# A decoder layer on one core: input statistics moved to the opening, six products by C on GpSimd, pieces of the last chunk a step sooner, and loops in a block that is skipped

## The chip, the cores and the metric

The kernel runs on one core of a Trainium2 chip. The metric is the device time of one execution in microseconds. TensorE (PE) multiplies matrices into PSUM, VectorE (DVE), ScalarE (ACT) and GpSimd (POOL) work on rows of 128 partitions, and SyncE (SP) issues the DMAs here. The engines run on their own and wait for each other by semaphores alone.

## What is computed

One decoder layer on 2048 tokens of width 256, in float32:

```python
x = x + attn_ref(layernorm(x))        # a Mamba block, then RMS norm, a gelu FFN, RMS norm
x = x + xattn_ref(layernorm(x), ctx)  # cross attention, 16 heads, 1601 keys
x = x + ffn_ref(layernorm(x))         # soft mixture of 8 experts with 128 slots each
```

The Mamba block has 512 channels and 16 states each. Its core is

```python
dA = exp(delta[..., None] * A)
h = dA * h + (delta * u)[..., None] * B[:, None, :]
y = einsum('bdn,bn->bd', h, C) + u * D
```

The cross attention is softmax(q k^T / 4) v with q and k of 16 numbers a head. The kernel shifts all scores by one bound worked out from the lengths of q and k; if that bound is too loose (over 120), it works out a maximum for each query instead.

## The kernel before

**The loop.** Time is cut in 4 chunks of 512 tokens (c). A chunk has 32 steps, one for each pair of channel blocks (p) and state (n); a step's number over all chunks is w = 32 c + i, from 0 to 127, and w works on 128 partitions x 1024 columns (two channel blocks side by side). For each w:

- GpSimd, `scan_input(w)` (L648, the product in L662): du times B into `dbu[w % 3]` in SBUF, and from chunk 1 on one more column (L669). It waits until VectorE's product of step w - 3 is done.
- ScalarE, `decays(w)` (L848, exponentials in L856): two exponentials into two PSUM banks, of which there are two pairs (w % 2). Ahead of them stands `carry_over(w - 2)` (L837, copy in L843), which takes the last column of the state of step w - 2 and waits for VectorE's product of that step.
- VectorE, `scan(w)` (L1258, the scan in L1268): h = decay * h + input, written over the decays in PSUM; then `between(c, i)` (L1351), a fixed list of other work for step i; then `times_c(w)` (L1271, product in L1279): state times C into one of six SBUF buffers.
- TensorE, `add_states(j)` (L1938, matmuls in L1946): adds the states 2j and 2j + 1 by an identity matrix to the sum in PSUM, at step 2j + 3.
- SP loads B and C for two steps at a time (`load_b`, L546, `load_c`, L555), each spread over all partitions, when the buffer of two loads ago is free. In its queue also stand the store of the next chunk's B and C (`store_bc`, at i = 10 of a chunk) and stores of keys.

**Around the loop.** Each engine has a list, by i, of what else it does in a step, for other chunks: projections and convolution of chunk c + 1, output projection, norm and FFN of chunk c - 1. In chunk 0 keys and values of the attention are made (GpSimd's `key_rest`, L692), in the last chunk the queries of chunks 0 and 1. All of it is in program order, so an instruction that waits holds up everything behind it on its engine.

**Statistics of the input.** `norm_stats(c)` (L1172, four bn_stats in L1174), `norm_moments(c)` (L1176, four bn_aggr in L1180 and a memset) and `norm_variance(c)` (L1182, L1186) are VectorE's, `layer_norm_root(c)` (L645 inside) is GpSimd's, `input_shift(c)` (L1188, L1190) again VectorE's. For chunk 1 they stand in steps 1, 2 and 4 of chunk 0, for chunk c + 2 in steps 15, 16 and 20 of chunk c. All chunks use the same columns of `stat`, `mv`, `ve`, `rstd` and `crec`. Before the loop VectorE makes chunk 0's statistics, the convolution and the step size, ending with the first input.

**The last chunk.** At i = 16 TensorE turns h1 of chunk 2 (`turn_h1`); at i = 17 ScalarE copies it (`turned_h1`, L867). TensorE's `hidden` (L1992) runs two FFN blocks each at i = 17, 19, 21 and 24, ScalarE's gelus of them (L872) at 18, 20, 22 and 25. Gelu and Exp need different tables, so each change between them loads one (ACT_TABLE_LOAD). ScalarE's `turned_query` (L927) stands at i = 12 and 21.

**The loose bounds.** After the loop VectorE writes `loose` (L1518). TensorE, VectorE and SP each read it and run a block only if it is 1 (L2127, L1532, L604). In TensorE's block one loop runs over the 4 chunks, and what is inside (4 tiles x 16 heads x 4 matmuls) is written out. In VectorE's block a loop runs over the 16 tiles with 16 reductions written out. In the runs here `loose` is 0 and the blocks are skipped. Behind them the scores and the attention follow (L2156, L1101, L2169).

## Time and profile before

| what | value |
|---|---|
| median of 3 runs | 1351.25 us (1350.41 to 1352.27) |
| the profiled execution | 1352.97 us |
| its span in the profile | 1351.2 us |
| busy: TensorE, its weight loads, VectorE, ScalarE, GpSimd | 1224.3, 641.3, 744.7, 929.5, 384.4 us |
| mean granted TensorE clock | 0.958 of full speed |
| opening / loop / rest up to the attention | 0 to 40 / 40 to 613 / 613 to 682 us |
| attention / experts | 682 to 1097 / 1097 to 1351 us |

How to read it: times are in us from the span's start. A row of instructions in order of time gives start, duration, engine, line, operation, what is written and read, and in brackets the idle time of the engine ahead of it and what ended it. "issue" is a wait for which the profile shows no releaser. Matmuls overlap each other, and a float32 one counts as two. Register and branch instructions aren't counted as busy, so a jump shows as idle time. Idle time of an engine that isn't the late one costs nothing.

### The profile page before, as it was taken

What the parts mean: (1) busy time and instruction counts of PE and PEld (TensorE: products, weight loads), DVE (VectorE), ACT (ScalarE), POOL (GpSimd) and SP (SyncE); (2) the same over time, 40 slices, a digit from 0 to 9 for tenths busy, and PEclk for the clock granted to TensorE, in tenths of its full rate; (3) what the DMA queues carried; (4) which work ended last, traced back from release to release, by engine and by line L of the source; (5) the groups of instructions that cost most, each with busy time, mean ns of one, the idle gap of its engine ahead of it and who ended that gap; (6) DMA issues with size and microseconds to landing.
All of it is one profiled execution on the core that took longest, in us unless ns stands there. A gap on an engine that the chain in (4) does not pass through costs nothing.

```text
span 1351.2 us, 19337 instructions
## 1 busy us (share of the span) xinstructions
PE 1224.3 (91%) x7848; PEld 641.3 (47%) x7848; DVE 744.7 (55%) x829; ACT 929.5 (69%) x1213; POOL 384.4 (28%) x280
## 2 busy tenths in 40 slices
PE   8679987998978897899979999999999999999999
PEld 4234543444443453355623333333333345588988
DVE  4999999999999999983352001001001237640011
ACT  5867756677657854662379999999989967742300
POOL 2646766666556765750000000000001000000000
PEclk9789988999988998999979999999999999999999
DMA  6534665243324432449461000000000000203501
GB/s 183 176 110 122 230 219 192 94 152 128 111 86 144 133 131 106 160 151 256 104 166 25 1 2 2 1 2 1 2 2 1 1 32 0 94 1 161 244 16 47
DMA packets 43033, 128.02 MB, mean 95 GB/s; under 512 B 6103, under 2 KB 21400, under 8 KB 39545
## 3 DMA queue, kind: packets, MB, share of 16 engines
q1 hardware_dynamic: 42942, 126.75, 29.0%
q8 instruction: 64, 1.05, 0.3%
q14 instruction: 27, 0.22, 0.1%
HBM read 109.64 MB, written 17.09 MB: 94 GB/s over the span
## 4 chain that ended last, share of the span: by engine, by line
PE 41%; ACT 26%; DVE 22%; issue 9%; DMA 1%; DVEq 0%; SPq 0%; POOL 0%; ACTq 0%
ACT arena L1101 18%; DVE ps L1268 13%; PE ps L2169 4%; PE ps L2300 4%; PE ps L2343 4%; PE ps L2156 4%; PE ps L2228 4%; PE ps L1946 4%; DVE arena L1279 4%; PE ps L2007 3%; PE ps L1992 2%; PE ps L2318 2%; ACT ps L856 2%; PE ps L2331 2%; PE ps L1726 2%
## 5 line engine op out<-in xcount | busy, mean ns | idle before, releaser
L1101 ACT ACTIVATE arena<-ps,bound 128x1536 f32<-128x1536 f32 (+1 forms) x278 | 403.9, 1559 | 13.1 <-PE ps L2156 12.7
L662 POOL TENSOR_TENSOR arena<-arena 128x1024 f32<-128x1024 f32 x127 | 298.3, 2350 | 217.5 <-DVE arena L1279 181.8
L1268 DVE TENSOR_TENSOR_SCAN ps<-ps,arena 128x1024 f32<-128x1024 f32 x128 | 300.6, 2349 | 9.2 <-ACT ps L856 7.8
L2156 PE MATMUL ps<-arena 97*32 97x512 bf16 x3264 | 239.2, 385 | 18.8 <-ACT arena L1101 12.9
L1946 PE MATMUL ps<-arena,ident 128*128 128x512 f32 x512 | 238.3, 611 | 3.9 <-DVE arena L1279 3.9
L2169 PE MATMUL ps<-arena 128*32 128x512 f32 (+1 forms) x1664 | 227.5, 598 | 3.1 <-DVE arena L1587 2.6
L856 ACT ACTIVATE ps<-arena 128x512 f32<-128x512 f32 x256 | 166.2, 682 | 52.0 <-DVE arena L1279 47.6
L2156 PEld LDWEIGHTS ps<-arena 97*32 97x32 bf16 (+1 forms) x3264 | 84.0, 96 | 211.9 <-ACT arena L1101 125.4
L645 POOL TENSOR_TENSOR rstd<-ve,mhalf 128x4 f32<-128x4 f32 (+3 forms) x23 | 25.5, 1110 | 495.7 <-DVE ve L1559 421.5
L1279 DVE TENSOR_TENSOR arena<-ps,arena 128x1024 f32<-128x1024 f32 x128 | 156.0, 1219 | 9.5 <-DMA arena<-bc_scratch 1.9
L1946 PEld LDWEIGHTS ps<-arena,ident 128*128 128x128 f32 x512 | 99.5, 197 | 125.9 <-issue 119.1
L1587 DVE STREAM_TRANSPOSE arena<-ps 128x512 f32<-128x512 f32 x16 | 11.5, 717 | 206.9 <-PE ps L2169 206.9
L843 ACT ACTIVATE arena<-ps 128x2 f32<-128x2 f32 x96 | 16.4, 171 | 116.2 <-DVE arena L1279 116.2
L2169 PEld LDWEIGHTS ps<-arena 128*32 128x32 f32 (+1 forms) x1664 | 54.1, 111 | 48.0 <-DVE arena L1587 7.5
L1992 PE MATMUL ps<-arena 128*128 128x512 f32 x128 | 59.7, 614 | 14.7 <-ACT arena L872 7.6
L1546 DVE TENSOR_TENSOR xt<-xt,ps 128x512 f32<-128x512 f32 x8 | 5.5, 688 | 116.0 <-PE ps L2174 116.0
L1873 PE MATMUL ps<-arena 128*128 128x512 f32 x128 | 61.3, 625 | 6.5 <-ACT arena L772 3.7
L2007 PE MATMUL ps<-arena 128*128 128x256 f32 x256 | 58.4, 382 | 3.2 <-ACT arena L872 3.2
L2228 PE MATMUL ps<-arena 128*128 128x512 f32 x128 | 57.7, 593 | 0.4 <-ACT arena L1125 0.4
L2300 PE MATMUL ps<-arena 128*128 128x257 f32 x256 | 55.8, 380 | 0.0
L2343 PE MATMUL ps<-arena 128*128 128x256 f32 x256 | 55.4, 379 | 0.0
L2007 PEld LDWEIGHTS ps<-arena 128*128 128x128 f32 x256 | 47.9, 190 | 14.5 <-ACT arena L872 4.8
(205 smaller groups left out, 1384.2 us busy)
## 6 DMA issues: line engine op xcount, KB each, us to landing
arena<-bc_scratch SPq DMA_DIRECT2D x128, 512.0 KB, 4.2
arena<-in_mw SPq DMA_DIRECT2D x16, 1024.0 KB, 10.3
qx_scratch<-arena SPq DMA_DIRECT2D x48, 128.0 KB, 3.3
arena<-qx_scratch SPq DMA_DIRECT2D x4, 1536.0 KB
arena<-kx_scratch SPq DMA_DIRECT2D x1, 4803.0 KB
kx_scratch<-arena SPq DMA_DIRECT2D x36, 128.0 KB, 4.7
arena<-vx_scratch SPq DMA_DIRECT2D x1, 3328.0 KB
vx_scratch<-arena SPq DMA_DIRECT2D x6, 512.0 KB, 5.1
```

What stands on the lines that cost most here:

```text
L662: product = pool.tensor_tensor(dbu[:, w % DR], du[:, DP * p:DP * p + DP], over(bg[:, w // BG % 2, n % BG], DP), ALU.mult)
L856: act.activation(decay_bank(w, x), delta[:, d], ACT.Exp, scale=neg_a[:, d, n:n + 1]).then_inc(S["da_ready"], 1)
L1101: act.activation(flat(prob[k % PSLOTS])[0:n, 0:w], banks(SPAN * (k % 2), SPAN)[0:n, 0:w], ACT.Exp, bias=bound[0:n, 3:4], scale=HD ** -0.5) ...
L1268: dve.tensor_tensor_scan(decay_banks(w), decay_banks(w), flat(dbu[:, w % DR]), carry[:, DP * p, n:n + 1], ALU.mult, ALU.add).then_inc(S["s ...
L1279: dve.tensor_tensor(state(w), ps[:, 2 + DP * (w % 2):2 + DP * (w % 2) + DP, :], over(cg[:, w // BG % 2, n % BG], DP), ALU.mult).then_inc(S ...
L1946: last = mm(bank(x), ident[:, :], state(2 * j + s)[:, x], start=False, stop=(j % HP == HP - 1 and (j in SUMMED or s == 1)))
L2007: last = mm(acc, gate[:, f, tok(i)], w2[:, f], start=(f == 0), stop=(c == NC - 1 and f == FB - 1))
L2156: last = mm(ps[r:r + w, SPAN * (k % 2) + s % SPAN, :], kx[0:XR + 1, head, b * P + r:b * P + r + w], qx[0:XR + 1, c, head, :], start=True, ...
L2169: last = mm(ps[2 * HD * x:2 * HD * x + 2 * HD, 6, :], vx[0:n, b, G * g + x, :], prob[s // SPAN % PSLOTS][0:n, s % SPAN], start=(b == 0), s ...
L2228: last = mm(bank(2 * (t % 2) + n), xnt[:, t % 2, k], snt[DK * k + n], start=(k == 0), stop=(k == DK - 1))
L2300: last = mm(ps[:, 4 + x if x < 4 else x - 4, 0:DM + 1], lg[:, t, tok(x)], xn[:, t, :], start=(t == 0), stop=(t == TT - 1))
L2343: last = mm(ps[:, t % 8, 0:DM], cwt[:, t, tok(x)], eo[:, x], start=(x == 0), stop=(x == NE - 1))
```

## The change

Four things, in one diff.

1. The statistics of chunks 1 and 2 are made before the loop: VectorE runs `norm_stats`, `norm_moments` and `norm_variance` for both behind `conv_keep(0)`, with the wait for all of x ahead of them; GpSimd runs both roots before the loop. Each chunk now has columns of its own in the small arrays. Chunk 3's stay at steps 15 and 16 of chunk 1. The counts that wait for `prep_dve` go up by 2.
2. In steps 19, 50, 53, 66, 82 and 85 (`POOLED`) the scan writes its state over its input in `dbu` in SBUF, VectorE makes no product, and GpSimd multiplies by C, in its queue just ahead of its input for step w + 3. ScalarE's carry copy of such a step waits for the scan alone and reads `dbu`. A new semaphore `pc_ready` counts GpSimd's products, and whoever waited for `hc_ready` waits by the two counts `by_vector` and `by_pool`.
3. In the last chunk ScalarE's `turned_h1` stands at i = 16 instead of 17, its gelus at 17, 19, 22 and 25 instead of 18, 20, 22 and 25, its `turned_query` at 11 and 20 instead of 12 and 21; TensorE's `hidden` at 17, 18, 21 and 24 instead of 17, 19, 21 and 24.
4. In TensorE's block for loose bounds three loops are nested (chunk, tile, pair of heads) around two heads written out, 8 matmuls; VectorE raises `nm_ready` by 2 inside its own block for it.

```diff
-SUMMED = []
+POOLED = [19, 50, 53, 66, 82, 85]
...
+        def by_vector(w):
+
+            return w - by_pool(w)
+
+        def by_pool(w):
+
+            return sum(v < w for v in POOLED)
...
                 if q >= 2:
-                    sp.wait_ge(S["hc_ready"], BG * (q - 1))
+                    sp.wait_ge(S["hc_ready"], by_vector(BG * (q - 1)))
+                    if by_pool(BG * (q - 1)):
+                        sp.wait_ge(S["pc_ready"], by_pool(BG * (q - 1)))
...
-                if w >= DR:
-                    pool.wait_ge(S["hc_ready"], w - DR + 1)
+                if w >= DR and w - DR in POOLED:
+                    pool.wait_ge(S["pc_ready"], by_pool(w - DR + 1))
+                    if w - DR < NW_ALL - NU:
+                        pool.wait_ge(S["carry_done"], w - DR + 1)
+                elif w >= DR:
+                    pool.wait_ge(S["hc_ready"], by_vector(w - DR + 1))
...
+            def times_c(w):
+
+                n = step(w)[2]
+                pool.wait_ge(c_in[w // BG % 2], 16 * (w // BG // 2 + 1))
+                pool.wait_ge(S["y_acc"], w // 2 - RING + 1)
+                pool.wait_ge(S["scan_done"], w + 1)
+                pool.tensor_tensor(state(w), dbu[:, w % DR], over(cg[:, w // BG % 2, n % BG], DP),
+                                   ALU.mult).then_inc(S["pc_ready"], 1)
...
+            pool.wait_ge(S["vx_init"], 6)
+            for c in (1, 2):
+                layer_norm_root(c)
             for c in range(NC):
                 for i in range(NU):
                     w = c * NU + i
+                    if w - DR in POOLED:
+                        times_c(w - DR)
                     if w:
                         scan_input(w)
...
             def carry_over(w):
                 c, p, n = step(w)
-                act.wait_ge(S["hc_ready"], w + 1)
+                if w in POOLED:
+                    act.wait_ge(S["scan_done"], w + 1)
+                    last = dbu[:, w % DR, :, C - 1:C]
+                else:
+                    act.wait_ge(S["hc_ready"], by_vector(w + 1))
+                    last = ps[:, 2 + DP * (w % 2):2 + DP * (w % 2) + DP, C - 1:C]
...
-                    if i == (20 if more else 17) and c:
+                    if i == (20 if more else 16) and c:
                         turned_h1(c - 1)
...
-                    if i in (18, 20, 22, 25) and not more:
-                        hidden(c - 1, 2 * (18, 20, 22, 25).index(i))
+                    if i in (17, 19, 22, 25) and not more:
+                        hidden(c - 1, 2 * (17, 19, 22, 25).index(i))
...
-                        if i in (12, 21):
-                            turned_query(i // 21)
+                        if i in (11, 20):
+                            turned_query(i // 20)
...
                 dve.wait_ge(S["da_ready"], DP * (w + 1))
-                dve.tensor_tensor_scan(decay_banks(w), decay_banks(w), flat(dbu[:, w % DR]),
+                states = flat(dbu[:, w % DR]) if w in POOLED else decay_banks(w)
+                dve.tensor_tensor_scan(states, decay_banks(w), flat(dbu[:, w % DR]),
                                        carry[:, DP * p, n:n + 1], ALU.mult, ALU.add).then_inc(S["scan_done"], 1)
...
                 if c == 0:
-                    if i == 1:
-                        norm_stats(1)
-                    if i == 2:
-                        norm_moments(1)
-                        norm_variance(1)
                     if i == 4:
                         input_shift(1)
...
                 if c + 2 < NC:
-                    if i == 15:
+                    if i == 15 and c:
                         norm_stats(c + 2)
-                    if i == 16:
+                    if i == 16 and c:
...
             conv_keep(0)
+            dve.wait_ge(S["w_mamba"], 16 * 3)
+            for c in (1, 2):
+                norm_stats(c)
+                norm_moments(c)
+                norm_variance(c)
...
                 between(w // NU, w % NU)
-                times_c(w)
+                if w not in POOLED:
+                    times_c(w)
...
-                        if i in (17, 19, 21, 24):
-                            f = 2 * (17, 19, 21, 24).index(i)
+                        if i in (17, 18, 21, 24):
+                            f = 2 * (17, 18, 21, 24).index(i)
...
                 with pe.Fori(0, NC) as c:
-                    for i in range(CT):
-                        for h in range(NH):
-                            if h >= 2:
-                                pe.wait_ge(S["nm_ready"], (c * CT + i) * NH + h - 1)
-                            for j, (o, n) in enumerate(KCOLS):
-                                last = mm(ps[:, 4 * (h % 2) + j, 0:n], head_queries(0, XR, c, h, tok(i)), kx[0:XR, h, o:o + n],
-                                          start=True, stop=True)
-                            last.then_inc(S["ms_ps"], 1)
-                        pe.wait_ge(S["nm_ready"], (c * CT + i) * NH + NH)
+                    with pe.Fori(0, CT) as i:
+                        with pe.Fori(0, NH // 2) as g:
+                            for x in range(2):
+                                pe.wait_ge(S["nm_ready"], c * (CT * NH) + i * NH + g * 2 + x + 1)
+                                queries = qx[0:XR, bass.ds(c, 1), bass.ds(g * 2 + x, 1), bass.ds(i * P, P)]
+                                for j, (o, n) in enumerate(KCOLS):
+                                    last = mm(ps[:, 4 * x + j, 0:n], queries.rearrange("p a b c -> p (a b c)"),
+                                              kx[0:XR, bass.ds(g * 2 + x, 1), o:o + n].rearrange("p a b -> p (a b)"),
+                                              start=True, stop=True)
+                                last.then_inc(S["ms_ps"], 1)
+                        pe.wait_ge(S["nm_ready"], c * (CT * NH) + i * NH + NH + 2)
```

## Rows read from the trace of the kernel before

**Rows 1.** The page, busy us (share of the span) and instructions of each engine.

```profile
PE 1224.3 (91%) x7848; PEld 641.3 (47%) x7848; DVE 744.7 (55%) x829; ACT 929.5 (69%) x1213; POOL 384.4 (28%) x280
```

**Rows 2.** Stretches: length; busy (count) of PE, PEld, DVE, ACT, POOL; PE clock, DMA share, GB/s.

```profile
142.00:284.00 142.00, 119.26 (x323) 61.33 (x321) 139.95 (x111) 93.50 (x176) 93.21 (x63) 0.89 0.53 175
284.00:311.00 27.00, 21.87 (x50) 8.98 (x49) 25.05 (x17) 26.09 (x41) 16.72 (x13) 1.00 0.44 135
...
323.00:355.00 32.00, 31.72 (x108) 19.34 (x109) 30.30 (x21) 17.66 (x39) 21.58 (x17) 1.00 0.39 132
...
429.00:445.00 16.00, 16.00 (x39) 6.87 (x38) 15.63 (x11) 15.70 (x24) 11.34 (x9) 1.00 0.42 144
```

**Rows 3.** Scan, VectorE's product (ns min/median/max), GpSimd's (busy, mean ns | idle).

```profile
L1268 DVE TENSOR_TENSOR_SCAN ps<-ps,arena x128: 2342/2349/2359, 40.5 to 604.7; 128x1024 f32<-128x1024 f32 x128
...
L1279 DVE TENSOR_TENSOR arena<-ps,arena x128: 1199/1222/1227, 42.9 to 607.1; 128x1024 f32<-128x1024 f32 x128
...
L662 POOL TENSOR_TENSOR arena<-arena 128x1024 f32<-128x1024 f32 x127 | 298.3, 2350 | 217.5 <-DVE arena L1279 181.8
```

**Rows 4.** Chunk 0: TensorE in order of time, and the chain's last piece there.

```profile
92.64 0.60 PE L1742 MATMUL ps<-sel,arena 128*128 128x8 f32 x2 [7.00 <-ACT arena L781]
...
119.34 3.45 PE ps L1946 x8
```

**Rows 5.** The last chunk: TensorE in order of time, the chain's last addition, and a wait.

```profile
541.87 1.04 PE L1726 MATMUL ps<-ident,arena 128*128 128x128 f32 x8
...
551.39 5.40 PE L1992 MATMUL ps<-arena 128*128 128x512 f32 x8 [5.05 <-ACT arena L867]
...
605.96 7.08 PE ps L1946 x16
...
DVE ps L1268 <- ACT ps L856: 4.0, 4, 1.5
```

**Rows 6.** VectorE in steps 1 and 2, in order of time.

```profile
44.07 2.35 DVE L1268 TENSOR_TENSOR_SCAN ps<-ps,arena 128x1024 f32<-128x1024 f32 x1
46.32 1.38 DVE L1174 BATCH_NORM_STATS2 stat<-xt 128x6 f32<-128x256 f32 x4
...
48.74 2.35 DVE L1268 TENSOR_TENSOR_SCAN ps<-ps,arena 128x1024 f32<-128x1024 f32 x1
...
51.10 0.28 DVE L1180 BATCH_NORM_AGGREGATE mv<-stat 128x2 f32<-128x6 f32 x3
```

**Rows 7.** VectorE and GpSimd in step 16, in order of time.

```profile
120.85 2.04 DVE L1186 TENSOR_SCALAR ve<-mv 128x4 f32<-128x4 f32 x1
...
120.74 2.12 POOL L692 TENSOR_TENSOR arena<-arena 128x1024 f32<-128x1024 f32 x1
```

**Rows 8.** The opening: VectorE in order of time, and the stretch 25 to 30 us.

```profile
30.73 0.75 DVE L1443 TENSOR_SCALAR arena<-ps,chan 128x512 f32<-128x512 f32 x1 [4.69 <-ACT arena L982]
...
25.00:30.00 5.00, 4.32 (x10) 1.23 (x10) 0.96 (x3) 3.48 (x6) 0.00 (x0) 1.00 0.08 18
```

**Rows 9.** VectorE in step 20, in order of time.

```profile
139.90 1.22 DVE L1279 TENSOR_TENSOR arena<-ps,arena 128x1024 f32<-128x1024 f32 x1 [1.85 <-DMA arena<-bc_scratch]
```

**Rows 10.** VectorE in step 71, in order of time.

```profile
354.61 2.36 DVE L1268 TENSOR_TENSOR_SCAN ps<-ps,arena 128x1024 f32<-128x1024 f32 x1 [1.15 <-ACT ps L856]
```

**Rows 11.** VectorE's product of step 53 and ScalarE's copy behind it, in order of time.

```profile
283.31 1.23 DVE L1279 TENSOR_TENSOR arena<-ps,arena 128x1024 f32<-128x1024 f32 x1
...
284.57 0.17 ACT L843 ACTIVATE arena<-ps 128x2 f32<-128x2 f32 x1 [2.09 <-DVE arena L1279]
```

**Rows 12.** TensorE and VectorE around the skipped blocks, in order of time.

```profile
682.29 1.05 PE L2156 MATMUL ps<-arena 97*32 97x512 bf16 x8 [5.66 <-issue]
...
677.07 0.14 DVE L1518 TENSOR_SCALAR loose<-bound 1x1 int32<-1x1 f32 x1
...
686.13 0.69 DVE L1525 CAST arena<-arena 128x1024 bf16<-128x1024 f32 x1
687.51 0.17 DVE L1615 TENSOR_SCALAR ve<-sqs 128x8 f32<-128x8 f32 x1 [0.69 <-issue]
```

## What the change was expected to do

> **What bounds the kernel now.** I read the page's busy shares first, then the table of stretches, then the chain of work that ended last, and where the chain leaves VectorE I read the engines' instructions in order of time. The shares alone mislead: TensorE is busy 91% of the span and VectorE 55% [rows 1]. The table of stretches shows VectorE at 139.95 of 142 us between 142 and 284 us [rows 2]. That is the Mamba loop: 128 steps from 40.5 us (step 0) to 604.7 us (step 127), each a scan of 2.35 us and a product by C of 1.22 us on VectorE [rows 3], about 3.60 us from one scan's start to the next when nothing else stands between. GpSimd makes each step's input in 2.35 us and waits 181.8 us in all for VectorE's products [rows 3]; it has room. Four places in the loop are not VectorE's. ScalarE is full from 284 to 311 us (26.09 of 27.00) [rows 2], and once more from 429 us (15.70 of 16.00) [rows 2]. TensorE is full from 323 to 349 us (31.72 of 32.00 in the stretch to 355) [rows 2]. Chunk 0 has a handover from VectorE over ScalarE to TensorE before 92.64 us [rows 4]. And from 551 to 613 us TensorE is the chain [rows 5]. A cut on VectorE is worth its time only where VectorE, or what it hands to ScalarE, is the late one.
>
> **Statistics in the opening.** Removed from steps 1, 2, 15 and 16 of chunk 0, per chunk: four bn_stats (1.38 us together), four bn_aggr (three take 0.28 us) and two small ones, about 0.6 us beside the bn_stats [rows 6]. From scan start to scan start (44.07 to 48.74 us is the first of four such pairs [rows 6]) the steps lasted 4.67, 3.90, 4.68 and 5.76 us against 3.60, so 1.07 + 0.30 + 1.08 + 2.16 = 4.6 us of VectorE go. The last is large because of one row: a 4-column tensor_scalar of 0.17 us took 2.04 us, exactly until GpSimd's subtraction of 120.74 to 122.86 us was over [rows 7]; it had been held up.
> Added before the loop: the same work twice, 2 x 2.0 = 4.0 us. VectorE sits idle there for 4.69 us, from 26.03 to 30.73 us, waiting for ScalarE [rows 8]. Cost nil, with 0.6 us to spare; the new wait for the rest of x costs nothing, since the DMA engines moved hardly anything from 25 to 30 us (busy 0.08) [rows 8]. Without that cover it would be 4.0 us, but the next VectorE result is not needed before about 32 us, so a spill of 1 us stays hidden too. GpSimd's two more root instructions (1.0 us each) fall into its idle time before 40.4 us.
> How much of the 4.6 arrives: steps 1 and 2 give 1.07 + 0.30 = 1.4, and ScalarE, full from 52.8 to 74.0 us, starts that much sooner. From 92.64 us, released by ScalarE, TensorE is full until 122.79 [rows 4]; it moves by the same 1.4. In steps 15 and 16 VectorE gains 3.2 more, but then ScalarE is late: carry copy, table load and two exponentials for step 18 would end near 124.7 us, where that scan started at 127.5 us. That is 2.8, and B, C and step size of chunk 1 leave ScalarE about 2.9 us sooner. SP is queued behind that store; its load of C for steps 20 and 21 lands at 139.87, and VectorE waits 1.85 us for it [rows 9]. So the whole chunk gains what the load gains: **2.9 us**, bounded by 1.4 (TensorE's shift alone) and 4.6 (all of it).
>
> **GpSimd's product in steps 19, 50, 53, 66, 82 and 85.** VectorE loses a 1.22 us product and starts its next scan about 1.15 us sooner. GpSimd gains a 1024-column product, by its own row of the same shape 2.35 us [rows 3], queued ahead of its input for step w+3. That input then ends some 2.4 us before the scan that needs it (GpSimd idles about 1 us a step, and runs two steps ahead), so nothing on VectorE waits. It also now waits for ScalarE's carry copy of that step, which in steps 50, 53, 82 and 85 comes within 1 us of the scan. TensorE's addition of that state comes about 1.5 us later than a VectorE product would allow, and C's buffer is released that much later; both have a step of room.
> Step 19 gives nothing: step 20 waits for C anyway [rows 9]. Step 66 (333.5 us) gives nothing: TensorE is the chain there [rows 2], and VectorE already waits 1.15 us for ScalarE at step 71 [rows 10]. Steps 50 and 82 stand in VectorE's own stretches: 2 x 1.15. Steps 53 and 85 stand just ahead of the two full stretches of ScalarE: before, ScalarE's copy waited for the product (283.31 us, 1.23 long) and started at 284.57 us [rows 11]; it will start when the scan ends, at 283.25: 2 x 1.3. Sum **4.9 us**; bounds 2.3 (only 50 and 82) and 7.2 (all six). The trace has no scan that writes SBUF. VectorE's nearest rows, the product that writes SBUF (1.22) and the ones that wrote PSUM, give no difference for the destination; I take 2.35 us and price the other case below.
> [...] All 128 scans last 2.35 us, those under a GpSimd instruction too [rows 3], while the tensor_scalar was held [rows 7]. [...]
>
> **Pieces a step sooner.** TensorE turned h1 of chunk 2 at 541.87 us in 1.04 us, added a pair until 546.34, then stood idle 5.05 us until 551.39 [rows 5], because ScalarE copies the turned h1 only behind the decays of step 114, which wait for VectorE's 549.0. The change copies it behind step 113's decays (over at 544.4 us), so TensorE goes on at once. From there I worked the pieces through by the durations of the rows. The first two hidden blocks end at 550.0; ScalarE's gelus, behind the decays of step 114 as before, at 553.0; the next two blocks, now ahead of the skip product, at 556. The order then returns to what ScalarE allows: turned_query at about 566, hidden 4 and 5 until 569.5, hidden 6 and 7 from 578.6, query lengths at 587.4 where they ended at 590.64. From there TensorE has 22.2 us of its own until the last addition, ending at 609.6 us instead of 613.0 [rows 5]. That is **3.4 us**. The exposed waits of VectorE for decays (4.0 us in four places) [rows 5] shrink to about 1.5, which is not a second gain: TensorE is last. Lower bound 0 (table loads in another order eat it), upper bound 5.05 + 1.6 (the two smaller gaps) = 6.7 us.
>
> **Loops in the loose-bounds block.** The block isn't entered; it is jumped over. VectorE's flag is written at 677.21 us; TensorE's first score is at 682.29, with 5.66 us idle before it and no releaser named [rows 12]. So 5.08 us for reading the flag and jumping. VectorE does the same test before a small block (16 reductions in a loop) and idles 0.69 us [rows 12], with its read under the cast before it (0.69 us long). TensorE's read waits for the flag, so its test costs 0.69 to 1.38 us; I take 1.1. The body skipped has 64 head passes of 4 matmuls, each with a weight load, 512 instructions and more; afterwards 16 and their address arithmetic. Gain 5.08 - 1.1 = **4.0 us**, bounds 0 and 4.4. It is all on the path: ScalarE has nothing left to do before TensorE's first score. What comes next is bound by ScalarE's exponentials and moves as a whole. VectorE's first work on finished heads waited for TensorE before, so it has some room.
> [...]
> The added semaphore count on VectorE lies inside the block and costs nothing.
>
> **Sum.** 2.9 + 4.9 + 3.4 + 4.0 = 15.2 us. The profiled execution took 1352.97 us around a span of 1351.2; so the changed one would take 1337.8 with a span of 1336.0. The median of the runs shown is 1351.25, 1.72 less, so 1336.05: **1336.1 us**.
>
> **Rivals.** [...] 10%.
> (b) The last chunk gains nothing, ScalarE's table loads (1.28 us each) falling before decays that VectorE waits for: 1339.5. For it: ScalarE already delays four scans there. 12%.
> (c) The GpSimd products are swallowed, because ScalarE or TensorE is equally late at 284 and 429 us: 1336.1 + 4.9 = 1341.0. For it: VectorE and TensorE are within 1.15 us of each other at step 71 [rows 10]. 10%.
> (d) More comes through: 4.6 in chunk 0 and 6.7 at the end, 1336.1 - 1.7 - 3.3 = 1331.1. 9%.
> (e) Slower: the scan that reads and writes the same SBUF buffer is held behind the GpSimd input that runs beside it (2.35 us) and goes at half rate (another 2.35). Six scans then cost 28.2 us: 1364.3. It turns into a loss beyond 15.2 us over six scans, 2.5 us each. Against it: the constant 2.35 under GpSimd [rows 3]. 4%.
> The forecast itself 53%, and 2% for a mixture that ends near no change.
>
> **Range.** A measurement tells about 0.2%, 2.7 us, from no change. All cases but (e) and the mixture are faster by more than that: 94, 2 and 4%, which I set to 0.93, 0.03 and 0.04. The range goes from 1330.5, under (d), to 1342.5, over (a), (b) and (c).
>
> **What would show it.** Scans of 2.35 us in the six steps; the input of step w+3 done before its scan; bn_stats of chunks 1 and 2 between 26 and 30.7 us, and ScalarE's abs still at 30.0; scan 21 near 138 us instead of 141.0; step 54 some 5.2 us sooner; TensorE's hidden right behind the addition at step 113; TensorE's idle time before the first score 1 to 2 us. It fails if the scan is longer, if step 71 hasn't moved by about 5.3 us, or if the idle time before the first score stays at 5.

## The result, and the profile after

The changed kernel takes 1342.14 us in the median (1341.15 to 1343.38, four runs), the kernel before beside it 1351.76: ratio 0.9932, 95% interval 0.992 to 0.9944. A second measurement gave 1341.29 against 1351.54, ratio 0.9925 (0.9908 to 0.9941). So 9.6 to 10.3 us are gone, 0.7%, where 15.2 were forecast; the time lies just under the upper edge of the range, 1342.5.

The profiled execution took 1341.15 us around a span of 1339.3. Four groups of its lines answer to rows shown above. First the page's busy line [rows 1], with VectorE 7.6 us below and GpSimd 12.3 above before, and the scans by line [rows 3]: 122 write PSUM, six write SBUF.

```profile
PE 1228.4 (92%) x7848; PEld 647.2 (48%) x7848; DVE 737.1 (55%) x823; ACT 929.7 (69%) x1213; POOL 396.7 (30%) x286
```

```profile
L1294 DVE TENSOR_TENSOR_SCAN ps<-ps,arena x122: 2326/2348/2358, 39.1 to 596.2; 128x1024 f32<-128x1024 f32 x122
L1294 DVE TENSOR_TENSOR_SCAN arena<-ps,arena x6: 2331/2336/2342, 128.1 to 419.0; 128x1024 f32<-128x1024 f32 x6
```

VectorE in order of time, in the opening [rows 8], at step 20 [rows 9], and in steps 52 to 54: both chunks' statistics stand before 28.7 us, 0.69 us of the 4.69 idle ones are left, VectorE still waits for C, and scan follows scan without a product of 1.22 between them.

```profile
24.74 1.40 DVE L1199 BATCH_NORM_STATS2 stat<-xt 128x6 f32<-128x256 f32 x4
...
28.51 0.17 DVE L1210 TENSOR_SCALAR ve<-mv 128x4 f32<-128x4 f32 x1
29.37 1.42 DVE L1469 TENSOR_SCALAR arena<-ps,chan 128x512 f32<-128x512 f32 x2 [0.69 <-ACT arena L1007]
...
135.55 1.22 DVE L1305 TENSOR_TENSOR arena<-ps,arena 128x1024 f32<-128x1024 f32 x1 [2.50 <-DMA arena<-bc_scratch]
...
273.97 0.92 DVE L1215 SCALAR_TENSOR_TENSOR crec<-mv,rstd 128x4 f32<-128x4 f32 x1
274.81 1.21 DVE L1305 TENSOR_TENSOR arena<-ps,arena 128x1024 f32<-128x1024 f32 x1
275.95 2.33 DVE L1294 TENSOR_TENSOR_SCAN arena<-ps,arena 128x1024 f32<-128x1024 f32 x1
278.20 2.33 DVE L1294 TENSOR_TENSOR_SCAN ps<-ps,arena 128x1024 f32<-128x1024 f32 x1
```

TensorE in order of time, in the last chunk [rows 5] and before the first score [rows 12]: hidden follows the addition at once, the last additions end at 604.50 instead of 613.04, and 1.88 us of idle time are left of 5.66.

```profile
541.37 3.60 PE L1973 MATMUL ps<-arena,ident 128*128 128x512 f32 x8
544.80 7.03 PE L2019 MATMUL ps<-arena 128*128 128x512 f32 x16
...
597.37 7.13 PE L1973 MATMUL ps<-arena,ident 128*128 128x512 f32 x16
...
669.99 2.75 PE L2181 MATMUL ps<-arena 97*32 97x512 bf16 x24 [1.88 <-DVE bound L1546]
```

**Where the time went.** Scans mark the loop, so the two traces can be laid side by side by the starts of the same scans. Each line is the length of a stretch, in us, worked out from these starts.

| stretch | before | after | difference | forecast |
|---|---|---|---|---|
| start to scan 0 | 40.47 | 39.08 | -1.39 | 0 |
| scan 0 to 21 | 100.57 | 97.61 | -2.96 | -2.9 |
| 21 to 49 | 123.04 | 122.99 | -0.05 | 0 |
| 49 to 56 (products 50, 53) | 27.81 | 25.99 | -1.82 | -2.45 |
| 56 to 72 | 66.32 | 67.25 | +0.93 | 0 |
| 72 to 88 (products 82, 85) | 77.98 | 75.51 | -2.47 | -2.45 |
| 88 to 96 | 33.15 | 34.49 | +1.34 | 0 |
| 96 to 106 | 47.75 | 49.44 | +1.69 | 0 |
| 106 to 127 (pieces) | 87.61 | 83.81 | -3.80 | -3.4 |
| scan 127 to first score | 77.60 | 73.82 | -3.78 | -4.0 |
| first score to end | 668.89 | 669.35 | +0.46 | 0 |

The sum is -11.85, the difference of the two spans. That is more than the medians differ by: the profiled execution of before is the slowest of its runs and that of after the fastest, and 1.39 us of it is the opening, which no edit reaches before 24.7 us. Three parts came out at their places as forecast, 2.96, 3.80 and 3.78. The six GpSimd products gave 4.3 us by step 88 and lost 4.0 of it again by step 106. VectorE's five largest waits between 320 and 525 us (total, times, longest) show where:

```profile
DVE ps L1294 <- ACT ps L881: 2.2, 3, 1.6
DVE arena L1320 <- PE ps L1988: 1.4, 1, 1.4
DVE ps L1294 <- ACT arena L869: 1.2, 2, 0.7
DVE arena L1313 <- PE ps L1973: 0.7, 1, 0.7
DVE arena L1336 <- PE ps L2037: 0.7, 1, 0.7
```

Three of them wait for TensorE: the gate for the last addition (step 66), the residual sums for the feed-forward product (68) and for the out projection (104). The largest is for ScalarE's decays, 1.6 us of it at step 71, where it had been 1.15. And TensorE had done some of its work at half speed. The same eight matmuls, after the same 3.16 us of idle time, first in before and then in after:

```profile
307.57 3.70 PE L1992 MATMUL ps<-arena 128*128 128x512 f32 x8 [3.16 <-ACT arena L872]
```

```profile
301.35 6.61 PE L2019 MATMUL ps<-arena 128*128 128x512 f32 x8 [3.16 <-ACT arena L897]
```

The two stretches with their granted clock (the column before DMA share and GB/s), before, then after. The 0.77 and 0.87 are means over parts: in after the clock was 0.50 from 302 to 306 us and from 461 to 463, and 1.00 from 308 to 315 and from 465 to 470.

```profile
300.00:315.00 15.00, 11.84 (x28) 4.92 (x27) 13.56 (x10) 14.82 (x21) 7.61 (x6) 1.00 0.45 140
457.00:470.00 13.00, 11.05 (x33) 5.91 (x32) 12.76 (x11) 11.18 (x18) 8.55 (x8) 1.00 0.43 134
```

```profile
300.00:315.00 15.00, 13.65 (x25) 5.95 (x26) 14.35 (x11) 13.47 (x22) 8.62 (x7) 0.77 0.33 101
457.00:470.00 13.00, 10.99 (x39) 7.80 (x37) 12.76 (x14) 8.30 (x13) 8.80 (x7) 0.87 0.35 125
```

### The profile page after: what moved, and what is told of

It is laid out like the page before. It is cut to its first block, busy times and chain, and to the rows that moved or that the text cites. A ratio compares the mean times of both kernels' runs of the same rounds, so it can differ in the third digit from the quotient of the medians.

```text
span 1339.3 us, 19392 instructions
## 1 busy us (share of the span) xinstructions
PE 1228.4 (92%) x7848; PEld 647.2 (48%) x7848; DVE 737.1 (55%) x823; ACT 929.7 (69%) x1213; POOL 396.7 (30%) x286
## 4 chain that ended last, share of the span: by engine, by line
PE 45%; ACT 28%; DVE 17%; issue 8%; DMA 0%; DVEq 0%; POOL 0%; SPq 0%; ACTq 0%
ACT arena L1126 18%; DVE ps L1294 9%; PE ps L1973 5%; PE ps L2194 4%; PE ps L2034 4%; PE ps L2181 4%; PE ps L2325 4%; PE ps L2368 4%; PE ps L2253 4%; ACT ps L881 3%; DVE arena L1305 3%; PE ps L2343 2%; PE ps L2019 2%; PE ps L2356 2%; PE ps L1753 2%
## 5 line engine op out<-in xcount | busy, mean ns | idle before, releaser
L1294 DVE TENSOR_TENSOR_SCAN ps<-ps,arena 128x1024 f32<-128x1024 f32 x122 | 286.5, 2348 | 9.0 <-ACT ps L881 6.9
L1305 DVE TENSOR_TENSOR arena<-ps,arena 128x1024 f32<-128x1024 f32 x122 | 148.7, 1219 | 11.0 <-DMA arena<-bc_scratch 2.5
```

The costliest lines, as they stand in the source:

```text
L1294: dve.tensor_tensor_scan(states, decay_banks(w), flat(dbu[:, w % DR]), carry[:, DP * p, n:n + 1], ALU.mult, ALU.add).then_inc(S["scan_done ...
L1305: dve.tensor_tensor(state(w), ps[:, 2 + DP * (w % 2):2 + DP * (w % 2) + DP, :], over(cg[:, w // BG % 2, n % BG], DP), ALU.mult).then_inc(S ...
```

## The experiments

Two theories. **A**: each part is worth what its own place shows, and the parts add. **B**: in chunks 2 and 3 TensorE is nearly as late as VectorE, so what the products gain is kept only as far as TensorE's load and granted clock allow. A later rival blamed any further product on GpSimd as such.

### One part alone

Each of these is the kernel before with one part of the diff: the loops in TensorE's block, the statistics in the opening, the six products, the pieces. For example, the only difference that counts in the third:

```
+POOLED = [19, 50, 53, 66, 82, 85]
```

> The kernel before with the loops in TensorE's block for loose bounds alone. Both theories: the idle time of TensorE before its first score falls from 5.66 to about 1.9 us, as in the profile of the changed kernel, and the whole kernel gains 3.8 us (3.3 to 4.3). If it gains less than 2, something behind the jump (the slow TensorE clock at the start of the scores) gives it back.

> The kernel before with the statistics of chunks 1 and 2 in the opening alone. Theory A (what chunk 0 gains arrives at the end): 2.9 us less, step 21's scan about 3 us sooner, and the last scan too. Theory B (TensorE is nearly as late as VectorE in chunks 2 and 3 and its clock decides there): step 21 is 3 us sooner all the same, since that is before TensorE's stretches, and the last scan 1.5 to 3 us sooner, depending on where the granted clock falls.

> The kernel before with GpSimd's product by C in the six steps alone. Theory A, the sum of the prediction: 4.9 us less. Theory B: the scans of steps 51, 54, 83 and 86 come 1.1 to 1.3 us sooner each, but by step 71 and again by step 105 VectorE and ScalarE wait for TensorE, which has not moved as far; 0 to 2 us remain of 4.9 at the end.

> The kernel before with the pieces of the last chunk a step sooner alone. Both theories: nothing changes before step 108; TensorE's first hidden block of chunk 2 starts about 5 us sooner, its last addition ends 3.4 us sooner (0 to 6.7), and so does the kernel.

| alone | median (before 1351.70) | ratio, interval | at its place in its profile |
|---|---|---|---|
| loops | 1349.67 | 0.9983, 0.9974 to 0.9993 | -3.8 (scan 127 to first score) |
| statistics | 1349.64 | 0.9977, 0.9967 to 0.9988 | -3.7 (scan 0 to 21; -3.0 against the second profile of before) |
| products | 1348.47 | 0.9974, 0.9963 to 0.9984 | -4.2 (steps 49 to 106) |
| pieces | 1350.46 | 0.9985, 0.9974 to 0.9997 | -3.5 (scan 106 to 127) |

At their places the parts again come near the forecast sizes. The products bring 4.2 of 4.9, and alone they lose nothing by step 106, with TensorE's whole work in place. The medians show a third to three quarters of the places (2.0, 2.1, 3.2 and 1.2 us; by the ratios 2.3, 3.1, 3.5 and 2.0). The stretch before scan 0, where three of these kernels do what before does, differs between the profiles by 1.7 us, so the whole span of one profile against that of another can't be read to better than that. A place inside it can be read more closely, but not everywhere: scan 0 to 21 took 100.57 us in one profile of before and 99.96 in the other.

### Before and after once more, and one part undone

> The kernel before once more, unchanged, for the spread of its profile and time. Both theories expect a ratio of 1.000 within 0.2%. If the changed kernel's 1.38 us at the first scan step is nothing but a state of TensorE's clock in the opening, this second profile may show the first scan up to 1.5 us sooner than the first profile of the kernel before, with no edit at all, and clock stretches at half speed in other places than there.

> The changed kernel once more, unchanged. Its median was 9.6 us below the kernel before. Expected 9 to 10 us again. In its profile, theory B (what the four pooled products of chunks 1 and 2 gain on VectorE is given back where TensorE's additions, at half clock in the stretch, come late) expects the give-back at steps 66 to 71 and 88 to 105 to move or change size with TensorE's clock there; theory A (the give-back is a fixed cost of the change's order of work) expects it at the same steps and in the same size: 0.96 us before step 72, 1.34 by step 94, 1.45 by step 105.

> The changed kernel with no product by C on GpSimd (VectorE does all 128, as before); the other three parts stay. Theory A (parts add): the product part alone gave 3.3 us, so this is 3.3 us slower than the changed kernel, about 1345.4 us, 6.3 us below the kernel before. Theory B (in company the gain of the products is given back, since TensorE, ScalarE and VectorE are equally late by step 105 and the statistics have used up the slack): 0 to 1 us slower than the changed kernel, 1342 to 1343 us; the shift of step 112 against the kernel before stays at 4.3 to 4.7 us.

> The changed kernel with TensorE's block for loose bounds unrolled as before; the other three parts stay. By its own place (idle time before the first score 5.7 instead of 1.9 us) 3.8 us slower than the changed kernel, about 1345.9; by the loops' own timed run 2.1 us slower, about 1344.2. A gap in the profile of 3.8 us at the jump with a smaller one in the medians would say that the first figure depends on the execution that is profiled.

> The changed kernel with the last chunk's pieces where they stood before; the other three parts stay. By its own place (the shift grows by 3.5 to 3.8 us between steps 112 and 127) 3.6 us slower than the changed kernel, about 1345.1; by that part's own median 1.2 to 2.0 us slower, about 1343.

The products are undone by one line, the pieces and loops by their hunks of the diff:

```
-POOLED = [19, 50, 53, 66, 82, 85]
+POOLED = []
```

| kernel | median | ratio, interval | slower than after |
|---|---|---|---|
| before again | 1351.51 | 0.9999, 0.9988 to 1.0009 | |
| after again | 1341.29 | 0.9925, 0.9908 to 0.9941 | |
| without products | 1342.86 | 0.9941, 0.9928 to 0.9954 | 1.6 |
| without loops | 1343.73 | 0.9949, 0.9936 to 0.9962 | 2.4 |
| without pieces | 1345.19 | 0.9956, 0.9943 to 0.9969 | 3.9 |

The changed kernel repeats itself, in time and, stretch by stretch, in its profile within 0.5 us. In company the pieces are worth what their place says, and this difference alone is clear of the noise: the intervals of the other two kernels overlap with that of after again. The loops' 2.4 us stand against 3.9 at their place (77.71 and 73.82 us). The products' 1.6 us lie between A's 3.3 and B's 0 to 1 and decide nothing. Their place does: steps 49 to 106 take 252.63 us with them and 253.01 without, so 0.4 us are kept, where alone they took 248.79 against 253.01 before. The changed kernel's clock repeated itself too, so that its second profile couldn't test whether the loss moves with the clock.

### Taking TensorE's lateness away

Half of the feed-forward block's second product is left out for chunks 0 to 2, in a kernel with the six products and one without. Both compute less than the layer needs and serve for this comparison alone.

```
-                for f in range(h * FB // 2, (h + 1) * FB // 2):
+                for f in range(h * FB // 2, (h + 1) * FB // 2 if c == NC - 1 or h == 0 else h * FB // 2):
```

> The changed kernel, with half of the feed-forward block's second product left out for chunks 0 to 2 (8 of 16 matmuls of 128x256 for each tile, 1.8 us each time, four times: 7.2 us less of TensorE by step 104). Theory B (TensorE's queue is what VectorE waits for at steps 66 to 71 and 104, so the gain of the GpSimd products is given back) expects those waits gone, the shift of 7.5 us at step 88 kept past step 104, and a time some 3 us below the changed kernel, plus up to 3.6 us more where the tail's two such tiles lie on the path: 1334 to 1338 us. Theory A (the loss is not TensorE's) expects the shift at step 107 to stay near 5 us, and no more than the tail's share.

> The same kernel with half of that product left out, and no product by C on GpSimd. What the six products are worth is the difference to the kernel with the same work left out and the six products on GpSimd. Theory B: 4 to 4.9 us (four products of 1.15 to 1.30 us each on VectorE's path, all kept). Theory A: 1.6 us, what it was with TensorE's whole work in place.

1331.70 us with the products and 1335.11 without: 3.4 us, and no run of the first is as slow as any of the second. The time is below the 1334 to 1338 forecast, since the work left out behind the loop was worth more than assumed: scan 127 to first score takes 67.75 us instead of 73.82, 6.1 less where 3.6 at most were expected. Steps 49 to 106 take 247.72 and 252.02 us, so in the profile 4.3 us are kept instead of 0.4. VectorE's waits from 320 to 525 us in the first of the two, all there are:

```profile
DVE ps L1294 <- ACT arena L869: 0.8, 2, 0.5
DVE arena L1320 <- PE ps L1988: 0.7, 1, 0.7
DVE arena L1305 <- issue: 0.3, 1, 0.3
```

Two of the three waits for TensorE are gone and the third is halved; the wait for ScalarE's decays, 2.2 us, is gone with them. That is B's mechanism, shown: it is TensorE's lateness that takes the gain. Step 66 shows it too: steps 56 to 72 are now 1.43 us shorter with the products (63.98 against 65.41), where with TensorE's whole work they were 0.9 longer. Not all is kept even so: the products lead by 5.6 us at step 88 and by 4.3 at step 106. TensorE's clock differs between the two as well (0.87 and 1.00 from 457 to 470 us), so this pair doesn't tell TensorE's amount of work from its speed. The forecast of 4 to 4.9 was a little high in the median.

### What TensorE's clock does to it

Eight of the profiles, with the clock granted to TensorE in the two stretches and the length of the steps about it:

| kernel | clock 300 to 315 | steps 56 to 72 | clock 457 to 470 | steps 88 to 96 |
|---|---|---|---|---|
| before | 1.00 | 66.32 | 1.00 | 33.15 |
| products alone | 0.89 | 66.32 | 1.00 | 33.17 |
| without products | 0.89 | 66.32 | 1.00 | 33.14 |
| without loops | 0.89 | 66.31 | 0.87 | 34.43 |
| loops alone | 0.77 | 67.24 | 1.00 | 33.14 |
| after | 0.77 | 67.25 | 0.87 | 34.49 |
| after again | 0.78 | 67.23 | 0.87 | 34.47 |
| four products and 109, later residual (below) | 0.89 | 66.69 | 1.00 | 33.23 |

The loops alone touch nothing before 670 us and lose 0.92 us at steps 56 to 72 nevertheless, at 0.77; the kernel without loops has all the rest of the change and loses nothing there, at 0.89. So those 0.9 us follow the clock and not the edits. The kernel without loops lost them one stretch earlier instead: it took 26.95 us for steps 49 to 56, the changed kernel 25.99, and VectorE waited 1.1 us there for ScalarE's decays instead of 0.2. TensorE's clock just ahead was lower, as the rows show, first without loops and then in the changed kernel. Without the products 0.74 cost nothing there (27.83 us, before 27.81).

```profile
262.00:275.00 13.00, 9.86 (x23) 4.83 (x21) 12.87 (x10) 6.57 (x13) 10.72 (x8) 0.74 0.45 132
```

```profile
262.00:275.00 13.00, 9.90 (x27) 4.96 (x26) 12.87 (x13) 7.45 (x15) 11.41 (x10) 0.87 0.35 112
```

Half speed just before 457 us costs nothing in steps 88 to 96: before again had a clock of 0.80 from 440 to 457 (0.50 from 450 to 454) and took 33.15 us for them. It took 48.23 us for steps 96 to 106, though, 0.5 more than the first profile of before, with a wait of 0.4 us for TensorE's out projection.

At steps 88 to 96 the clock and the edits mostly come together: all nine profiles that have the six products and the statistics show 0.87 from 457 to 470 us. Three kernels have products on GpSimd and 1.00 there. The products alone and the last row of the table lose 0.1 us at most, the third (four products and the later residual, below) 0.7. The rows of this stretch for the first two:

```profile
457.00:470.00 13.00, 11.47 (x42) 7.54 (x41) 12.76 (x14) 8.80 (x15) 8.08 (x8) 1.00 0.50 156
```

```profile
457.00:470.00 13.00, 11.40 (x43) 7.63 (x42) 12.76 (x12) 8.61 (x14) 8.03 (x7) 1.00 0.48 161
```

The last kernel has the statistics, the loops, the pieces and TensorE's whole work. With its clock and without the wait at step 104 it keeps 3.9 us over steps 49 to 106 (249.13 against 253.01), so TensorE's amount of work alone doesn't force the loss.

### A later residual, and more products

The wait of 1.42 us at step 104 can be avoided by asking for TensorE's second half a step later, the mean and norm behind it one step later too.

```
-                    first_residual(c - 1, 1)
+                if i == 9 and not more:
+                    first_residual(c - 1, 1)
...
-                if i == 14 - 4 * last and c:
+                if i == 14 - 3 * last and c:
...
-                if i == 17 - 5 * last and c:
+                if i == 17 - 4 * last and c:
```

> The changed kernel with one VectorE step moved: in the last chunk the second half of the residual addition, which waits 1.42 us for TensorE's out projection at step 104, one step later, and the mean and norm behind it one step later too. Theory B: the wait is gone, and VectorE keeps 1.0 to 1.4 us up to the end of the loop, about 1340 us; if the hidden product of the last chunk starts later for it (it follows the norm), nothing of that is lost, since TensorE has gaps there. Rival: scan 105 waits as long for its decays or its input as it now waits for TensorE, then 0 us.

> The version with the second half of the residual addition one step later in the last chunk, once more. If the first median (1338.7, ratio 0.9909) was its real time, 0.990 to 0.992 again; by its place (1.5 us at steps 103 to 106, kept to the end unless TensorE is the bound there) about 0.9915 to 0.992. In the profile, steps 103 to 106 take 18.1 us, and steps 56 to 72 and 88 to 96 take 66.3 and 33.2 us where TensorE's clock there is 0.89 or more, 67.2 and 34.4 where it is lower.

> The same version with the products by C of steps 19 and 66 back on VectorE, which in the changed kernel gained nothing, so four on GpSimd. Expected the same time within 0.3 us if those two are worth nothing (steps 0 to 21 then 0.3 to 0.8 us longer by the profiles that lack that of step 19, with TensorE's later clock stretches elsewhere), a ratio of 0.990 to 0.993.

This version is the fastest of the kernels that compute the whole layer: 1338.69 (ratio 0.9909, 0.9896 to 0.9922), again 1338.78 (0.9906, 0.989 to 0.9923), and with the products of steps 19 and 66 back on VectorE 1338.36 (0.9907, 0.9892 to 0.9922). The intervals overlap with those of the changed kernel, but three measurements agree within 0.4 us. Steps 103 to 106 take 18.13 to 18.16 us instead of 19.65, and the wait for L1988 there is gone. That is 1.5 us at the place and 2.5 to 3 in the median; why it is more isn't known. Products 19 and 66 are worth nothing that the medians can show, as forecast. The clock's case: the first run has 0.89 and 0.87 with 66.32 and 34.18 us, the second 0.77 and 0.87 with 67.26 and 34.51, both as the table has it. The third has 0.89 and 1.00 with 66.66 and 33.82, which is between the two kinds and spoils a clean rule.

More products on GpSimd in the last chunk were meant to add to this:

```
-POOLED = [19, 50, 53, 66, 82, 85]
+POOLED = [19, 50, 53, 66, 82, 85, 105, 108]
```

> The changed kernel with two more products by C on GpSimd, those of steps 105 and 108 of the last chunk, where GpSimd stands still for 3.7 us before its next input. If VectorE alone sets the pace from step 105 to the end of the loop, each gives 1.15 us and keeps it: 2.3 us less, about 1339 us. If the give-back is a property of every such product (ScalarE and TensorE equally late), 0 to 0.5 us.

> The changed kernel with one more product by C on GpSimd, that of step 109, where VectorE does nothing but scans and products for the three steps that follow. With steps 105 and 108 on GpSimd VectorE's step_size took 3.17 us instead of 1.23 and the four products of the norm 5.98 instead of 1.78, each beside a GpSimd product. If that collision is the whole loss, this one gives 1.15 us by step 113 and keeps it up to step 117, where TensorE's hidden product and additions have no gap until the end of the loop: between 0 and 1.2 us less than the changed kernel, 1340.3 to 1341.5. If every further product on GpSimd costs time in the last chunk, it is slower than the changed kernel.

> The changed kernel with the second half of the residual addition a step later in the last chunk, and the products by C of steps 50, 53, 82, 85 and 109 on GpSimd (those of 19 and 66, which gained nothing, back on VectorE). If what was gained at step 104 (1.6 us) and at step 109 (1.15 us) adds up, 1338 to 1339 us, ratio 0.990 to 0.991; if TensorE in the last chunk is the bound from step 117 on, as with the residual step alone, 1338.7 to 1340.

The first should have brought 2.3 us and was slower than the changed kernel by about 4: 1345.55, ratio 0.9954 (0.9942 to 0.9966). VectorE in order of time, and GpSimd beside it:

```profile
511.48 3.18 DVE L1258 TENSOR_TENSOR arena<-arena 128x1024 f32<-128x1024 f32 x1
...
525.03 5.98 DVE L1330 SCALAR_TENSOR_TENSOR arena<-arena,rstd,scales 128x256 f32<-128x256 f32 x4
```

```profile
510.25 3.33 POOL L692 TENSOR_TENSOR arena<-arena 128x1024 f32<-128x1024 f32 x1
...
525.62 2.60 POOL L692 TENSOR_TENSOR arena<-arena 128x1024 f32<-128x1024 f32 x1
528.30 2.43 POOL L676 TENSOR_TENSOR arena<-arena 128x1024 f32<-128x1024 f32 x1
```

The same two in the changed kernel's second profile, with GpSimd still:

```profile
509.58 1.23 DVE L1258 TENSOR_TENSOR arena<-arena 128x1024 f32<-128x1024 f32 x1
...
522.50 1.78 DVE L1330 SCALAR_TENSOR_TENSOR arena<-arena,rstd,scales 128x256 f32<-128x256 f32 x4
```

1.95 + 4.20 = 6.15 us lost against the 2.3 priced would make 3.85, and steps 96 to 127 of the two profiles differ by 3.71: the whole of it. These VectorE instructions, with two inputs in SBUF, were held until GpSimd's was over, while scans beside GpSimd kept their 2.33. These holds are no waits for a semaphore: no idle time stands ahead of the two, and the instructions themselves last longer, 3.18 us for 1.23 and 5.98 for 1.78. The forecast had used the hold of [rows 7] for the scan alone. With step 109 alone the gain of 1.1 us by step 110 is there. At step 112 it is lost to the next such group, which took 4.14 us instead of 2.44 since GpSimd's input had been pushed under it (1342.41, ratio 0.9936, 0.9923 to 0.9948, above the 1340.3 to 1341.5 forecast):

```profile
540.98 4.14 DVE L1374 TENSOR_SCALAR arena<-xt,mv,rstd 128x256 f32<-128x256 f32 x4
```

Joined to the later residual it was my own error of placement: the norm, moved to step 109, fell under the product of 109 and took 5.94 us instead of 1.78, and 1342.68 (0.9933, 0.992 to 0.9946, forecast 1338 to 1340) gave back what the residual had brought. So neither theory's number for more products held; the collision decides.

### What the jump costs in a timed run

```
+            for jump in range(4):
-            with pe.If(pe.value_load(loose[0:1, 0:1], min_val=0, max_val=1) > 0):
+                with pe.If(pe.value_load(loose[0:1, 0:1], min_val=0, max_val=1) > 0):
```

> The kernel before, with TensorE's unrolled block for loose bounds standing four times one behind the other, each jumped over. If each jump stalls TensorE for 3.5 to 4.1 us, in a timed run as in a profiled one, the last scan to the first score takes 77.6 + 3 times 3.7 to 4.2 = 89 to 90 us, and the time is 11 to 12.6 us above the kernel before, 1363 to 1364. If timed runs pay less for a jump than a profiled one (2.3 us each, as the loops' medians say), the profile still shows 89 to 90 us there, and the median is only some 7 us above, about 1358.5.

```profile
702.86 2.75 PE L2157 MATMUL ps<-arena 97*32 97x512 bf16 x24 [26.72 <-issue]
```

1370.06 us in the median, 18.8 above before (ratio 1.0136, 1.0121 to 1.0151); in the profile the last scan to the first score takes 98.67 us, 21.1 more. Three more jumps cost 7.0 us each in the profile and 6.3 in the median, not 3.7 to 4.2: both numbers missed. Each of them also reads the flag and tests it again, which the forecast had left out; how much of the 7.0 us that is wasn't measured. But timed runs pay nine tenths of what the profile shows, so a jump that is cheaper when timed doesn't explain why the loops' median effect is 2.0 to 2.4 us and not 3.8.

## Why the prediction was right or wrong

**Statistics in the opening: right.** 2.96 against 2.9, hidden before 28.7 us, and the wait for C at step 20 moved and didn't go, as worked out.

**Pieces: right.** Hidden started behind the addition at once; 3.6 us from step 113 on and 3.8 from 106, against 3.4; 3.9 in the median in company.

**Loops: right at the place.** The idle time before the first score is 1.88 us, inside the 1 to 2 forecast, and 3.78 us went against 4.0. The jump over 512 and more instructions of TensorE stands with 5.66 us of idle time, the one over 8 matmuls, their weight loads and the address arithmetic with 1.88. Why the longer one costs more, and from what length on, wasn't tested. Rival (a), at 10%, in which the 4.0 us don't come (1340.1), didn't happen at the place. In the median 2.0 to 2.4 us were seen.

**The GpSimd products: wrong, and this is the step that failed.** Forecast 4.9, kept 0.3 to 0.4 in the profile and 1.6 in the median, which isn't clear of the noise. The scans held their time: 2336 ns in the middle where they wrote SBUF, 2348 where they wrote PSUM. The forecast's rows for this weren't there, since in the trace of before VectorE writes PSUM by its scans alone. Steps 50, 82 and 85 gave what was priced; steps 19 and 66 gave nothing at their places, as forecast. Two steps of the working failed. The smaller: at step 52 a 4-column instruction with two SBUF inputs took 0.92 us instead of 0.34 beside GpSimd, although [rows 7] had shown such a hold. That is its row before, and GpSimd's instruction beside it after:

```profile
279.46 0.34 DVE L1190 SCALAR_TENSOR_TENSOR crec<-mv,rstd 128x4 f32<-128x4 f32 x1
```

```profile
272.52 2.35 POOL L676 TENSOR_TENSOR arena<-arena 128x1024 f32<-128x1024 f32 x1
```

The larger: I let every microsecond from steps 50 to 85 pass to the end. [Rows 2] and [rows 10] had TensorE full from 323 to 349 us and VectorE 1.15 us from the edge at step 71; I used that for step 66 and not for what comes before it. [Rows 2] also had TensorE busy for 16.00 of 16.00 us from 429 us on, where I named only ScalarE as full. In chunk 3 the same block of TensorE work stands before step 104, and I hadn't looked there. And the sum had no term for TensorE's clock: 0.93 us at steps 56 to 72 follow it, and of the 1.34 at steps 88 to 96 kernels with 1.00 there lose between 0 and 0.7. So the outcome is nearest to rival (c), 1341.0, to which I gave 10%; TensorE was among the engines it named, its places weren't right: at 284 and 429 us the gain came through, and it was given back behind each.

GpSimd's idle time was put at about 1 us a step; by [rows 3] it is 217.5 us over 127 inputs, 1.7, which changed nothing.

One sign of failure stayed silent by luck. Step 71 was to move by about 5.3 us and moved by 5.29, but 1.39 of that is the opening, which no edit explains.

**The sum.** 15.2 - 4.6 for the products = 10.6 by the places, against 9.6 and 10.3 in the medians. Against the forecast of 1336.1 the median is 6.0 us late. In the span 3.35 of 15.2 us are missing, mainly 4.6 for the products less 1.39 by the luck of the opening. The other 2.7 are the step from the profiled execution to the median. The forecast took 1.72 off for it, as in before, but the changed kernel's profiled execution was 0.99 faster than its median. The range had no term for this step.

**Open.** Why loops and pieces alone show 2.0 and 1.2 us in the median, where their places show 3.8 and 3.5: 0.9 of the loops' is seen at steps 56 to 72. The rest is seen in no profile, and a profile is one execution. Even behind the first score, where no edit does anything, the profiles of the later residual took 670.76 and 666.51 us and that of the changed kernel 669.35. All five kernels that have the statistics and show 1.00 from 457 to 470 us lack the products of steps 19 and 66, so TensorE's speed there seems to follow what is done earlier; by what way wasn't tested.

## What to carry over

A gain made ahead of a stretch in which a second engine is full is kept only as far as that engine comes sooner too, so follow the shift through every such stretch to the end, and price its clock at both levels there (1.00 and 0.50 here), from rows of each. Before moving work to GpSimd, list VectorE's instructions with all inputs in SBUF that will run beside it (1.23 us became 3.18 and 1.78 became 5.98 here, where scans kept 2.33), and also those beside the GpSimd work that is pushed back. Look for waits that can be moved: moving one by a step brought 1.5 us at its place here, where six products moved to another engine left 0.3.

## What the runs showed of the hardware

TensorE's granted clock in the opening differs from execution to execution, in code that is the same. From 10 to 17 us, before again, after, and the later residual:

```profile
10.00:17.00 7.00, 6.17 (x15) 2.93 (x15) 1.58 (x7) 2.35 (x4) 0.00 (x0) 0.76 1.10 329
```

```profile
10.00:17.00 7.00, 6.17 (x19) 3.00 (x19) 3.09 (x9) 3.35 (x6) 0.00 (x0) 1.00 1.12 322
```

```profile
10.00:17.00 7.00, 6.17 (x14) 2.93 (x14) 1.75 (x8) 1.97 (x4) 0.00 (x0) 0.62 1.09 325
```

Scan 0 starts at 40.33, 39.08 and 42.28 us in these. In all three TensorE had been equally busy, 6.17 of 7 us, and at 0.76 and 0.62 it did 15 and 14 matmuls for 19. The last two have the same opening, so that is 3.2 us between two executions before the loop has begun, as much as a whole part of the change.

Reading a flag and jumping over a block of 512 and more instructions of TensorE left it idle for 5.66 us once, and three more such blocks behind the first added 7.0 us each on average. The 3.8 us that the loops save are only the difference to a small block in the same place, which left 1.88 us.

TensorE's half speed doesn't always cost time. A clock of 0.74 from 262 to 275 us (0.50 from 268 to 272) cost nothing with all products on VectorE (27.83 us for steps 49 to 56, 27.81 before at 0.87). With two of them on GpSimd the same steps took 26.95 us at 0.74 and 25.99 at 0.87.
